# State product of a Mamba-2 block in three products of rounded parts, moved between two projections of the next block

## The reference

```
log_a = A_c * dt_c; cum_log_a = cumsum(log_a)
y_intra = einsum(L, C·B, dt, x)                      # within a chunk
decay_to_end = exp(chunk_log_decay - cum_log_a)
state_local = einsum('bcjGH,bcjGH,bcjGn,bcjGHp->bcGHnp', decay_to_end, dt, B, x)
state_at_end = scan: state = chunk_decay * state + state_local
y_inter = einsum(decay_from_start, C, state_at_start)
out = x + ((y_intra + y_inter + D*x) * silu(gate)) @ out_proj_w
```

## Time and profile before

| | us |
|---|---|
| median of 3 runs | 2304.61 (2303.82 to 2307.62) |
| the profiled execution | 2305.35 |
| its span, first to last instruction | 2303.6 |
| PE busy | 2252.9 (98%) |
| DVE, ACT, POOL busy | 1363.3, 882.4, 693.7 |

### The profile page before, as it was taken

One profiled execution on the slowest core, in us unless ns is written; L12 is line 12 of the kernel. 1 busy time (PEld: TensorE's weight loads), 2 busy tenths in 40 slices (PEclk: granted clock), 3 DMA queues, 4 the chain that ended last, 5 costly groups with the idle time before them and its releaser, 6 DMA issues.

```text
span 2303.6 us, 41271 instructions
## 1 busy us (share of the span) xinstructions
PE 2252.9 (98%) x16412; PEld 2003.2 (87%) x16412; DVE 1363.3 (59%) x3201; ACT 882.4 (38%) x1563; POOL 693.7 (30%) x534
## 2 busy tenths in 40 slices
PE   6999999999998999999999999999999999999998
PEld 6999998777798899999998999998999999777787
DVE  6777762222228677777777777778777763223322
ACT  5232321233327555554555555455323231223321
POOL 1244443112220433233332223331144444122222
PEclk9999999999999999999999999999999999999999
DMA  8776525989844111111111111104376532988949
GB/s 273 263 260 209 164 84 181 306 282 284 236 89 138 45 30 36 28 28 29 28 28 29 28 28 29 28 22 169 125 282 224 199 104 78 312 291 286 290 83 183
DMA packets 129279, 334.73 MB, mean 145 GB/s; under 512 B 24450, under 2 KB 45186, under 8 KB 118400
## 3 DMA queue, kind: packets, MB, share of 16 engines
q1 hardware_dynamic: 80592, 236.63, 28.7%
q0 software_dynamic: 48496, 95.46, 18.1%
HBM read 218.25 MB, written 172.77 MB: 170 GB/s over the span
## 4 chain that ended last, share of the span: by engine, by line
PE 87%; DVE 4%; ACT 4%; DMA 3%; issue 1%; SPq 0%; DVEq 0%; POOL 0%; ACTq 0%; POOLq 0%
PE m_p_ab L1687 3%; PE m_p_x L1687 3%; PE m_p_x L1689 3%; PE m_p_x L1688 3%; PE m_p_ab L1689 3%; PE m_p_ab L1688 3%; PE p_up_b L769 3%; PE p_x_b L873 3%; PE p_x_a L873 3%; PE p_up_a L769 3%; PE p_gate_b L769 2%; PE m_p_y L1808 2%; PE m_p_y L1809 2%; PE p_up_b L771 2%; PE p_up_b L770 2%; PE p_gate_b L770 2%
## 5 line engine op out<-in xcount | busy, mean ns | idle before, releaser
L2004 DVE SCALAR_TENSOR_TENSOR m_xt<-m_ssm,m_convw,m_xt 128x256 f32<-128x256 f32 x384 | 211.9, 565 | 55.2 <-ACT m_ssm L1553 46.0
L1687 PE MATMUL m_p_ab<-m_ht_hi,m_wi_b_hi 128*128 128x256 f32 x576 | 164.5, 286 | 3.8 <-ACT m_ssm L1553 3.4
L506 POOL DMA_INDIRECT slot_rows<-a_hr,a_slot_now x128 | 128.4, 1003 | 131.3 <-PE p_gate_a L771 81.0
L506 POOL DMA_INDIRECT slot_rows<-b_hr,b_slot_now x128 | 128.9, 1007 | 129.5 <-PE p_gate_b L771 80.1
L1688 PE MATMUL m_p_ab<-m_ht_lo,m_wi_b_hi 128*128 128x256 f32 x576 | 161.3, 280 | 0.0
L1689 PE MATMUL m_p_ab<-m_ht_hi,m_wi_b_lo 128*128 128x256 f32 x576 | 161.2, 280 | 0.0
L769 PE MATMUL p_gate_a<-a_hts_hi,a_w_hi 128*128 128x256 f32 x512 | 148.4, 290 | 1.8 <-DVE a_hts_lo L1068 1.8
L1457 POOL TENSOR_TENSOR m_state_dec<-m_state,m_etot 128x1024 f32<-128x1024 f32 x31 | 74.0, 2386 | 248.7 <-ACT m_etot L1569 248.7
L769 PE MATMUL p_gate_b<-b_hts_hi,b_w_hi 128*128 128x256 f32 x512 | 147.0, 287 | 0.3 <-DVE b_hts_lo L1068 0.3
L769 PE MATMUL p_up_a<-a_hts_hi,a_w_hi 128*128 128x256 f32 x512 | 145.5, 284 | 0.0
L769 PE MATMUL p_up_b<-b_hts_hi,b_w_hi 128*128 128x256 f32 x512 | 145.4, 284 | 0.0
(11 more groups left out here) (378 smaller groups left out, 7346.7 us busy)
## 6 DMA issues: line engine op xcount, KB each, us to landing
a_ew<-in_ew SPq DMA_DIRECT2D x32, 1536.0 KB, 7.2
b_ew<-in_ew SPq DMA_DIRECT2D x32, 1536.0 KB, 7.3
after_ffn<-a_zeros POOLq DMA_DIRECT2D x6, 2048.0 KB, 9.2
out<-b_zeros POOLq DMA_DIRECT2D x6, 2048.0 KB, 10.1
slot_rows<-a_zeros POOLq DMA_DIRECT2D x1, 8336.0 KB, 37.1
a_rows<-slot_rows SPq DMA_DIRECT2D x32, 260.5 KB, 8.4
b_rows<-slot_rows SPq DMA_DIRECT2D x32, 260.5 KB, 8.2
m_x<-after_ffn SPq DMA_DIRECT2D x16, 512.0 KB, 3.6
```

Of the source, the lines that this page charges most:

```text
L506: g_.indirect_dma_start(out=xg, out_offset=bass.IndirectOffsetOnAxis(ap=slot_now[r % HR][:, at:at + 1], axis=0), in_=hr[r % HR][:, j, :], ...
L1687: t.matmul(out, l_hi, r_hi_, start=first, stop=False)
L2004: ins_ = v.scalar_tensor_tensor(xt[:, m, :], ssm[:, m, i:i + BM], convw[:, m, i:i + 1], xt[:, m, :], ALU.mult, ALU.add)
```

## The change

The state product becomes three products of rounded parts. New are, per tile, xs_hi (ACT copy of xs, 128x1024) and xs_lo (DVE, in place of xs), and per block btok_hi (ACT copy of the B tokens, 128x256) and btok_lo (DVE, in place). xs_hi lies where decay of tile 0 lies, so ACT waits for `y_full` before it writes it; btok_hi lies where cb lies and waits for `decay_ready`. In all but the last block `state_product(n, 0)` stands between the C and B projections of block n+1 instead of ahead of the dt projection; in the last block it stands behind the second FFN's first transposes instead of ahead of them. The semaphores soft_exp and dtt_set are dropped; their waits go by soft_ready and pick_ready.

```diff
+        btok_lo = Region(nc, "m", tok_at)("btok_lo", [P, TM, P], F32R)
         cum_rows = sb("cum_rows", [P, BM], F32R)
+        btok_hi = Region(nc, "m", sb.next)("btok_hi", [P, TM, P], F32R)
         cb = sb("cb", [P, TM, P])
...
         cdec_both = sb("cdec", [P, TM, NH, P])
+        xs_hi = Region(nc, "m", sb.next)("xs_hi", [P, NH, HP], F32R)
         decay_both = sb("decay", [P, TM, NH, P])
+        xs_at = sb.next
         xs, state = sb("xs", [P, NH, HP]), sb("state", [P, NH, HP])
+        xs_lo = Region(nc, "m", xs_at)("xs_lo", [P, NH, HP], F32R)
...
+            def b_hi(n):
+                act.wait_ge(ab_free, n * JOBS + J_TOK + 1)
+                act.wait_ge(decay_ready, n * TM + TM)
+                a.activation(btok_hi[:], btok, ACT.Copy).then_inc(b_hi_ready, 1)
+
+            def state_in_hi(n, j):
+                act.wait_ge(xs_ready, n * TM + j + 1)
+                if j == 0:
+                    act.wait_ge(y_full, n * TM + 1)
+                else:
+                    act.wait_ge(s_full, n * TM + j)
+                a.activation(xs_hi[:], xs[:], ACT.Copy).then_inc(xs_hi_ready, 1)
...
                 if not is_(n, NM - 1):
                     turned(n + 1)
+                    b_hi(n)
+                    state_in_hi(n, 0)
                     head(n + 1)
+                    state_in_hi(n, 1)
                 else:
+                    b_hi(n)
+                    state_in_hi(n, 0)
                     phase.follow.act.early(1)
...
             def state_product(n, j):
-                pe.wait_ge(xs_ready, n * TM + j + 1)
+                pe.wait_ge(xs_lo_ready, n * TM + j + 1)
...
+                hi, lo = (part[:, :, :].rearrange("p h q -> p (h q)") for part in (xs_hi, xs_lo))
                 for b in range(2):
-                    mm = t.matmul(p_cr[:, b, :], btok[:, j, :],
-                                  xs[:, :, :].rearrange("p h q -> p (h q)")[:, b * 512:(b + 1) * 512],
-                                  start=True, stop=True)
+                    cols = slice(b * 512, (b + 1) * 512)
+                    mm = three(p_cr[:, b, :], btok_hi[:, j, :], btok_lo[:, j, :], hi[:, cols], lo[:, cols], True, True)
                 mm.then_inc(s_full, 1)
...
-            def head(n):
+            def head(n, between=None):
                 pe.wait_ge(ht_ready, n * 2 + 2)
                 project_dt(n)
                 project(n, J_C, C0)
+                if between:
+                    between()
                 project(n, J_B, B0)
...
                 y_product(n, 0)
-                state_product(n, 0)
                 if not is_(n, NM - 1):
-                    head(n + 1)
+                    head(n + 1, lambda: state_product(n, 0))
                     y_product(n, 1)
                     state_product(n, 1)
                     to_tokens(n + 1)
                 else:
                     pe.wait_ge(cleared, CLEARED)
                     phase.follow.pe.early(0)
+                    state_product(n, 0)
                     y_product(n, 1)
...
+            def b_lo(n):
+                dve.wait_ge(b_hi_ready, n + 1)
+                v.tensor_tensor(btok_lo[:], btok, btok_hi[:].bitcast(F32), ALU.subtract)
+
+            def state_in_lo(n, j):
+                dve.wait_ge(xs_hi_ready, n * TM + j + 1)
+                v.tensor_tensor(xs_lo[:], xs[:], xs_hi[:].bitcast(F32), ALU.subtract).then_inc(xs_lo_ready, 1)
...
                         norm_rest(n + 1)
+                    b_lo(n)
+                    state_in_lo(n, 0)
                     skip_part(n, 0)
                     if more:
                         add_state(n, 0)
                         gated(n, 0)
+                        state_in_lo(n, 1)
                     else:
                         add_state(n, 0)
```

More of the change, by code:

```diff
@@ L1272, in mamba @@
         cum_t = Region(nc, "m", early)("cum_t", [NH, BM])
+        tok_at = sb.next
         tok = sb("tok", [P, TM * P + TM * NH])
         btok = tok[:, 0:TM * P].rearrange("p (j n) -> p j n", j=TM)
+        btok_lo = Region(nc, "m", tok_at)("btok_lo", [P, TM, P], F32R)
         dtraw = tok[:, TM * P:]
@@ L1347, in mamba @@
         nabs_ready, soft_ready, la_ready = sem("nabs_ready"), sem("soft_ready"), sem("la_ready")
-        soft_exp, dtt_set = sem("soft_exp"), sem("dtt_set")
+        b_hi_ready, xs_hi_ready, xs_lo_ready = sem("b_hi_ready"), sem("xs_hi_ready"), sem("xs_lo_ready")
         pick_ready, cum_t_ready, cum_hi_ready, cum_lo_ready = (
@@ L1528, in head @@
                 if is_(n, 0):
-                    act.wait_ge(dtt_set, 1)
+                    act.wait_ge(pick_ready, 1)
                 copy_job(n, J_DT, dtt[0:CR, :], CR)
@@ L1537, in tokens_out @@
                 copy_job(n, J_TOK, tok[:, :])
+            def b_hi(n):
[9 more added lines that the diff above has]
+                a.activation(xs_hi[:], xs[:], ACT.Copy).then_inc(xs_hi_ready, 1)
             def softplus(n):
                 act.wait_ge(nabs_ready, n + 1)
-                a.activation(nabs[:], nabs[:], ACT.Exp).then_inc(soft_exp, 1)
-                act.wait_ge(soft_exp, n + 1)
+                a.activation(nabs[:], nabs[:], ACT.Exp).then_inc(soft_ready, 1)
+                act.wait_ge(soft_ready, 2 * n + 1)
                 a.activation(nabs[:], nabs[:], ACT.Ln, bias=c.ones[:, 0:1]).then_inc(soft_ready, 1)
@@ L1660, in early @@
                     ones2 = c.ones[:, :].unsqueeze(1).to_broadcast([P, TM, P])
-                    a.activation(dtt[:].rearrange("p (j t) -> p j t", j=TM), ones2, ACT.Copy, scale=0.0).then_inc(dtt_set, 1)
+                    a.activation(dtt[:].rearrange("p (j t) -> p j t", j=TM), ones2, ACT.Copy, scale=0.0)
                     a.activation(cum_rows[:].rearrange("p (j t) -> p j t", j=TM), ones2, ACT.Copy, scale=0.0)
@@ L1963, in decay_steps @@
             def decay_steps(n):
-                dve.wait_ge(soft_ready, n + 1)
+                dve.wait_ge(soft_ready, 2 * n + 2)
                 dve.wait_ge(cr_full, n * TM)
```

## The result

The changed kernel takes **2320.84 us** (median of 6 runs, 2318.51 to 2325.53), the kernel before beside it 2305.62 (6 runs, 2303.82 to 2307.62): a ratio of 1.0068, with a 95% interval of 1.0055 to 1.0081. So it is 15.2 us slower. Forecast were 2327.6, range 2308 to 2336. The profiled execution took 2319.08 us (span 2317.4), 13.7 more than the profiled one of before.

The account below looks back on a forecast made before the run. The prediction took PE, busy 98% of the span, to bound the kernel. To the profiled 2305.35 us it added 20.7 for 15 blocks and 2.3 for the last, less 0.74: 2327.6 us, range 2308 to 2336.

Parts of the forecast that it names:

- PE saves 0.34 per product: State product on PE: six rounded matmuls take 1.38 us instead of 1.72; 31 products, 10.5 us if nothing waits.
- Waits of 0.50 and 0.37 to 0.39 ahead of tile 0's product and of the second y product: PE waits 0.50 us for tile 0's xs_lo, then 0.37 to 0.39 for DVE's add_state before the second y product.
- Wait of 0.99 ahead of tile 1's product: PE waits for tile 1's xs_lo, held on DVE by POOL's state_dec taking its turn first; 0.99 us, bounds 0 to 1.76.
- from DVE's end to PE's start is 0.26: Handover before state products: PE starts 0.26 us after DVE ends, read from the last block's second y product.
- 1.38 per block, 20.7 in 15 blocks: Out product starts later in each block, by 1.36 to 1.40 us, taken as 1.38; 15 blocks give 20.7.
- Last block, 2.3: Last block, once: second y product starts at 1583.13 against 1580.86, behind conversions and add_state; 2.3 us lost.
- The cover behind: Later skip part and softplus chain still leave 1.5 us before cumulate; rival that it is used up: 2335.1 us, chance 0.12.
- that POOL does not get its turn: Rival: tile 1's xs_lo gets in ahead of state_dec; 0.3 us lost per block, time 2311.4, chance 0.19.
- the case in which the sum of waits stays under the saving: Rival: a block's three waits total under 0.68 us, so it is faster; without waits 10.5 saved, 2294.1, chance 0.10.

Follow-up runs that it names:

- tile-1-only kernel: Rounded parts for tile 1's product only, tile 0's product plain in its old place, against the changed kernel: 2297.77 us, ratio 0.9961; repeated 2300.10 us, ratio 0.9973.
- POOL's order alone: Changed kernel with one edit: POOL's state_dec of tile 1 waits until DVE has made xs_lo of tile 1; 2313.63 us, ratio 1.0038.
- the rounding at the old place: Changed kernel with tile 0's product back ahead of the dt projection, rounded parts kept; 2351.52 us, ratio 1.0205.
- both versions with xs_hi over h: Changed kernel with xs_hi laid over tile h: 2317.63 us, ratio 1.0045; also with POOL's state_dec of tile 1 behind xs_lo: 2307.39 us, ratio 0.9993.
- the last block plain: Changed kernel with the last block's product plain and in its old place, no parts made there; 2322.12 us, ratio 1.0061.
- the move alone: Kernel before with tile 0's plain state product moved between the C and B projections, nothing rounded; 2311.64 us, ratio 1.0028.
- the scaling in a gap: Against all waits away: DVE's scaling for the next block moved behind the second half, where DVE waits for the softplus; 2293.18 us, ratio 0.9945.
- all waits away: Changed kernel with xs_hi over h, state_dec behind xs_lo, tile 0's product mid-C, last block plain, DVE's scaling behind y_lo of tile 0; 2323.76 us, ratio 1.0062.

## Why the prediction was right, and where it was off

- *PE saves 0.34 per product*: right where PE does not wait: the tile-1-only kernel's period is 0.31 to 0.34 shorter. Behind a wait the first step takes 0.34 and the product 1.49 to 1.50 instead of 1.72, so 0.22 saved; the forecast had 0.25.
- *Waits of 0.50 and 0.37 to 0.39 ahead of tile 0's product and of the second y product*: right in sum, with the split moved. Measured from the y product's start, C is over at 5.89, the product starts at 6.21 (0.32 waited), and B would be over at 9.07, if it took as long as before, where the y product starts at 9.61 (0.54 waited): 0.86 together, forecast 0.87. DVE's chain sets the second start, so a product that starts earlier only waits later.
- *Wait of 0.99 ahead of tile 1's product*: right in mechanism, too large in size; this is the term that was mis-sized. It was 0.64: the y product is over at 13.18 and the product starts at 13.82. The turns of 1.08 and 1.75 came as worked out, and POOL's order alone takes the wait to nothing. What failed is the step "from DVE's end to PE's start is 0.26". That price came from the y product behind the state add and still holds for it: 1158.37 + 1.21 = 1159.58, PE at 1159.84. Ahead of the state product it is 0.06: 1155.16 + 1.22 = 1156.38, PE at 1156.44, and 1161.20 + 2.79 = 1163.99, PE at 1164.05. It enters twice. The first product starts 0.18 earlier than forecast, which, with a product 0.02 longer, puts POOL and with it the end of the second xs_lo 0.16 earlier; and the second handover itself is 0.20 shorter: 0.36 of the 0.37 missing. Waits of 0.86 and 0.64, less two savings of 0.22, are the 1.06.
- *Why the handovers differ*: not by the form of the matmul. The changed kernel's trace has both prices at one line, ahead of the same float32 transposition (DVE's a_hr ends at 23.00, a_htr_lo at 29.01):

```profile
21.55 1.45 DVE L1004 TENSOR_SCALAR a_hr<-a_xr,a_mv,a_rstd 128x512 f32<-128x512 f32 x3
23.06 0.66 PE L825 MATMUL p_x_a<-ident,a_hr 128*128 128x128 f32 x4 [0.29 <-DVE a_hr L1004]
...
28.33 0.68 DVE L1010 TENSOR_TENSOR a_htr_lo<-p_x_a,a_htr_hi 128x512 fp32r<-128x512 f32 x1
29.16 0.66 PE L825 MATMUL p_x_a<-ident,a_hr 128*128 128x128 f32 x2 [5.43 <-DVE a_htr_lo L1010]
```

  What goes with the price is the number of semaphores that the trace names ahead of the matmul: one for the first transposition and the state product, two for the second transposition, five for the y product, whose code has five waits in a row. Over all waits of PE for DVE or ACT of more than 0.1 us in the twelve traces it is 0.05 to 0.06 us with one semaphore, 0.14 to 0.15 with two to four, whatever the matmul, and 0.25 to 0.29 with five, which only the y product has. No run changed the number alone, so the cause itself is argued and not shown.
- *1.38 per block, 20.7 in 15 blocks*: measured 1.06 at the out product of block 7, and 1.03 x 15 = 15.4 by the periods. This is the largest part of the 6.8 us by which the forecast was too high.
- *Last block, 2.3*: 2.21 in its place. That the whole shows it is not settled, see below.
- *The cover behind*: right. la of the next block ended 1.3 to 1.4 us ahead of `cumulate`, forecast 1.5; the kernel with the scaling moved showed what happens once that is gone.
- *The rivals*: that POOL does not get its turn is refuted by the xs_lo of 2.79, and its price was right: with POOL's order a block loses 0.34 (53.87 to 54.21), forecast 0.3; the tile-1-only kernel shows the case in which the sum of waits stays under the saving, and is faster.

**What stays open.** 15.4 + 2.2 = 17.6 us are lost in the blocks of the profiled runs and 0.6 ahead of them, and the profiled runs differ by 13.7. So 4.5 us came back behind the second y product of the last block, in the second feed-forward stage, where the code is the same: from there to the end of the span it is 722.8 us before and 718.3 after. Part of it is an event of the one execution: the clock of before was low there for a while (same columns), and that of the changed kernel was not.

```profile
1600.00:1605.00 5.00, 3.03 (x16) 2.48 (x15) 3.80 (x7) 3.28 (x4) 0.00 (x0) 0.89 0.75 258
1605.00:1610.00 5.00, 5.00 (x33) 4.82 (x33) 2.65 (x3) 1.05 (x3) 0.00 (x0) 0.77 0.65 224
```

```profile
1619.00:1624.00 5.00, 3.03 (x25) 2.64 (x24) 4.05 (x5) 3.41 (x4) 0.00 (x0) 1.00 0.92 311
```

A clock of 0.89 and 0.77 over 5 us each is 1.7 us of matmul lost. The rest is within what this last part varies by in the other traces (718.9 to 722.2 us, the rounding at the old place left out). But the medians show it too: they differ by 15.2, 2.4 less than 17.6. Tile 1 alone in both its runs, both versions with xs_hi over h and the last block plain are also 2.3 to 2.8 us below what their periods and last blocks give, while POOL's order alone and the move alone are 0.9 and 0.4 above it; the two extremes are the scaling in a gap, 5.7 below, and all waits away, 3.5 above. The cause was not separated, and so a difference of a few microseconds between medians is not explained to the last by the periods.

## What to carry to other kernels

Before a matmul is made cheaper by splitting its inputs, lay out the chain that makes the parts, with both elementwise engines in it, and ask what PE does meanwhile: here the saving was there from the start, 0.22 us per product behind a wait and 0.34 without one, and 1.50 us of waits per block ate it. Where DVE and POOL both work out of SBUF, the order in which they get their turns is part of the schedule: one wait in POOL's queue gave back 0.69 us a block, and a scaling moved under a POOL instruction cost 1.3 a block against the same scaling in a gap. A handover read off one row holds for that row's waits: take it from a row with the same waits ahead of it. A single tile whose parts were ready in time was already a gain, and should have been the first thing to try.

## What the runs showed of the hardware

- The handover from DVE's end to PE's start was 0.06 us ahead of the state product and 0.26 ahead of the y product in the same block; over twelve traces it went with the number of semaphores named ahead of the matmul (one: 0.05 to 0.06, two to four: 0.14 to 0.15, five: 0.25 to 0.29), and float32 and rounded matmuls had the same.
- DVE and POOL took turns, a whole instruction each: a held DVE instruction of 128x1024 ended 1.08 us after POOL's, a held POOL instruction 1.75 us after DVE's. POOL's turn put behind xs_lo brought xs_lo from 2.79 to 1.23 us.
- After 2.5 us of idle time in a stream that is otherwise full, the granted clock fell to 1.2 GHz for 3.4 us behind 10 of 15 waits, and cost 1.55 us each time. The same idle time in the other blocks cost nothing more.
- A DVE instruction with a single SBUF tensor as input, the scaling of x, was held by POOL too: 2.58 us for the pair against 1.00.
